# Pre-norm state-space layer and top-1 expert layer on one core: one of four tiles of each block turned by DMA, three steps placed elsewhere

## The reference

```python
x = L0_attn_x                                    # (2, 4096, 512)
n = layernorm(x)
s = sigmoid(silu(n @ s_w1.T + s_b1) @ s_w2.T + s_b2)
u = (n @ B_w.T + B_b) * s                        # (2, 4096, 128)
h_t = h_{t-1} @ A.T + u_t                        # scan over 4096 steps
y = h @ C_w.T + C_b + n @ D_w.T + D_b
x1 = x + y * sigmoid(n @ g_w.T + g_b)
m = layernorm(x1)
e = argmax(m @ gate_w.T)                         # one of 8 experts per row
out = x1 + m + m @ expert_w[e].T
```

## Time and profile before

| what | value |
|---|---|
| median of 3 timed runs | 926.9 us (925.25 to 929.12) |
| profiled execution: its own time | 928.0 us |
| its span, mean granted TensorE clock | 926.3 us, 0.996 |
| TensorE busy | 904.1 us (98%) |
| VectorE busy | 704.2 us (76%) |
| ScalarE busy | 597.2 us (64%) |
| GpSimd busy | 389.8 us (42%) |
| chain that ended last | 88% TensorE, 3% VectorE, 1% ScalarE |

### The profile page before, as it was taken

How to read it: one execution, slowest core, us unless ns; L and a number is a source line. 1 busy time by engine, 2 the same in 40 slices (tenths; PEclk the granted TensorE clock), 3 DMA queues, 4 the chain that set the end, 5 groups by cost and what they waited for, 6 DMA issues and landing times.

```text
span 926.3 us, 15829 instructions
## 1 busy us (share of the span) xinstructions
PE 904.1 (98%) x4565; PEld 739.5 (80%) x4566; DVE 704.2 (76%) x1725; ACT 597.2 (64%) x826; POOL 389.8 (42%) x492
## 2 busy tenths in 40 slices
PE   8999999999999999999999999999999999999995
PEld 7777888888888888888888888888868887888884
DVE  6778979788888979788888979788787465555552
ACT  5568676857767675867767685857534345666661
POOL 1032536181634536181634527181623453333432
PEclk9999999999999999999999999999999999999998
DMA  8435384746657474748557485846789868999881
GB/s 311 131 91 140 89 206 114 205 108 171 151 140 187 89 198 120 204 111 171 153 137 186 90 199 118 206 113 178 254 275 413 336 234 243 224 218 219 192 187 39
DMA packets 203593, 165.55 MB, mean 179 GB/s; under 512 B 128245, under 2 KB 161781, under 8 KB 202496
## 3 DMA queue, kind: packets, MB, share of 16 engines
q1 hardware_dynamic: 192576, 130.89, 55.6%
q0 software_dynamic: 10800, 33.70, 10.7%
q10 hardware_dynamic: 144, 0.07, 0.0%
HBM read 81.63 MB, written 54.68 MB: 147 GB/s over the span
## 4 chain that ended last, share of the span: by engine, by line
PE 88%; DVE 3%; issue 2%; SPq 1%; ACT 1%; DMA 1%; POOL 0%; ACTq 0%; DVEq 0%; POOLq 0%
PE y L1662 19%; PE y L1382 7%; PE y L1383 7%; PE y L1384 7%; PE gates L1382 7%; PE gates L1384 6%; PE gates L1383 6%; PE scan L1527 3%; PE turned L1568 3%; PE gates L1568 3%; PE scan L1382 2%; PE scan L1383 2%; PE scan L1384 2%; PE turned L1650 2%; PE scores L1484 2%
## 5 line engine op out<-in xcount | busy, mean ns | idle before, releaser
L1662 PE MATMUL y<-experts,x1T_hi 128*128 x568 | 180.7, 399 | 2.6 <-issue 2.5
L578 POOL TENSOR_SCALAR ln_var_eps<-ln_mean_var 128x4 f32<-128x4 f32 x16 | 3.6, 224 | 302.3 <-DVE ln_mean_var L1017 302.2
L1662 PEld LDWEIGHTS y<-experts,x1T_hi 128*128 128x128 f32 x568 | 103.4, 188 | 24.1 <-issue 4.2
L623 POOL DMA_INDIRECT out<-gate,ids x71 | 72.0, 1015 | 111.1 <-DVE gate L1347 68.2
L1662 PE MATMUL y<-experts,x1T_lo 128*128 x284 | 111.4, 392 | 0.0
L1347 DVE TENSOR_TENSOR gate<-y,raw_weights 128x512 f32<-128x512 f32 x71 | 49.1, 691 | 75.6 <-PE y L1662 50.4
L1382 PE MATMUL gates<-GwT_hi,xT_hi 128*128 128x512 f32 x256 | 104.6, 409 | 0.0
L1382 PE MATMUL y<-DwT_hi,xT_hi 128*128 128x512 f32 x256 | 101.8, 398 | 0.5 <-DVE gateT L939 0.5
L731 ACT ACTIVATE joined<-flipped 128x1024 uint16<-128x1024 uint16 x60 | 82.3, 1371 | 29.7 <-DVE xT_lo L1167 21.1
L1383 PE MATMUL y<-DwT_lo,xT_hi 128*128 128x512 f32 x256 | 100.3, 392 | 0.0
L1384 PE MATMUL y<-DwT_hi,xT_lo 128*128 128x512 f32 x256 | 100.3, 392 | 0.0
(11 more groups left out here) (276 smaller groups left out, 2340.9 us busy)
## 6 DMA issues: line engine op xcount, KB each, us to landing
raw_weights<-routed_rows SPq DMA_DIRECT2D x71, 258.0 KB
x_in<-L_attn_x SPq DMA_DIRECT2D x32, 512.0 KB, 5.0
x_rows<-L_attn_x SPq DMA_DIRECT2D x32, 512.0 KB, 4.9
turned_experts<-raw_weights SPq DMA_DIRECT2D x32, 512.0 KB, 5.3
experts<-turned_experts SPq DMA_DIRECT2D x8, 2048.0 KB
raw_weights<-L_ffn_expert_w SPq DMA_DIRECT2D x32, 256.0 KB, 3.1
routed_rows<-padrow SPq DMA_DIRECT2D x9, 258.0 KB
out<-gate,ids POOLq DMA_INDIRECT x71
```

What stands on the lines that cost most here:

```text
L623: nc.gpsimd.indirect_dma_start(out=out_rows, out_offset=bass.IndirectOffsetOnAxis(ap=ids[r][:, 0:1], axis=0), in_=res[r], in_offset=None, ...
L1662: ins = nc.tensor.matmul(Y[m % 2][:], x2T[a][:, k, m % 2 * P:(m % 2 + 1) * P], flat[:, bass.ds(first + (w * KD + k) * D, D)], start=(k == ...
```

## The change

In the bodies of blocks 2 to 14 (the tails of blocks 1 to 13):

- Tile 3 of x1 is no longer turned by TensorE. ScalarE splits it in planes (`halve_x1`), SyncE issues one more DMA transpose ahead of the next block's flips, ScalarE joins it (`join_x1`), and `tail_hi` and `tail_lo` read the joined tile in SBUF instead of a PSUM bank.
- On TensorE the first pair's last four score products stand alone; the second pair's products and `tail_back` move behind `to_middles` and behind the last `y_dense`; `over(b, 3)` to `over(b, 5)` and the products around them change places.
- `gates(b-1, 3)` of ScalarE moves behind the first sigmoid of the silu; `join(b+1, 2)` moves behind the copies of h.
- `ln2_stats` of tile 3 moves up to stand ahead of `over(b, 0)`; `gate_sum(b, 1)`, `tail_lo(b-1, 3)`, `low(b+1, 0)` and `low_piece(b, 0)` move down.
- `add_identity` moves from VectorE to GpSimd, behind `scatter` (from block 1's body on).

```diff
+        def by_dma(b, i):
+
+            return 0 < b < LASTB - 1 and i == NT - 1
+        x1_halves = yb[:, 0, :].bitcast(u16)
+        x1_flipped = yb[:, 2, :].bitcast(u16).rearrange("p (c t) -> p c t", t=P)
+        x1_joined = yb[:, 0, :]
...
+                if by_dma(b - 1, NT - 1):
+                    sp.wait_ge(S_["x1_halves"], b - 1)
+                    sp.dma_start_transpose(x1_flipped, x1_halves).then_inc(x1_turned, 16)
...
+            def add_identity(b, j):
+
+                f = expert_piece(b, j)[1]
+                pool.wait_ge(w_loaded[j], 16 * (b + 1))
+                part = w_raw[j][:, f * P:(f + 1) * P]
+                nc.gpsimd.tensor_tensor(part, part, ident[:], ALU.add).then_inc(w_ident[j], 1)
...
+                if 0 < b < LASTB:
+                    for j in range(2):
+                        add_identity(b + 1, j)
...
+            def halve_x1(b, i):
+
+                act.wait_ge(S_["x1_ready"], NT * b + i + 1)
+                nc.scalar.activation(x1_halves.rearrange("p (h d) -> p h d", h=2), planes(xrow[b % 2][:, i, 0:D]), ACT.Copy
+                                     ).then_inc(S_["x1_halves"], 1)
+
+            def join_x1(b, i):
+
+                act.wait_ge(x1_turned, 16 * b)
+                nc.scalar.activation(planes(x1_joined), x1_flipped.rearrange("p (h k) t -> p h (k t)", h=2), ACT.Copy
+                                     ).then_inc(S_["x1_joined"], 1)
...
-                    gates(b - 1, NT - 1)
...
+                    if tail and m == 0:
+                        gates(b - 1, NT - 1)
...
+                if dma:
+                    halve_x1(b - 1, 3)
...
+                if dma:
+                    join_x1(b - 1, 3)
+                    tail_hi(b - 1, 3)
...
+                if dma:
+                    gates(b, 1)
                 if tail:
                     scoresT(b - 1, 1)
-                gates(b, 1)
...
-                    join(b + 1, 2)
+                    if not dma:
+                        join(b + 1, 2)
...
+                if dma:
+                    ln2_stats(old, oldq, 3)
                 over(b, 0)
...
-                if tail and ahead:
-                    for j in range(2):
-                        add_identity(b + 1, j)
                 over(b, 3)
-                gate_sum(b, 1)
+                if not dma:
+                    gate_sum(b, 1)
                 over(b, 4)
+                if dma:
+                    gate_sum(b, 1)
...
+                if dma:
+                    tail_lo(old, 3)
...
+                elif tail:
+                    for n in range(KD, 2 * KD):
+                        score_product(b - 1, 0, n)
...
+                else:
+                    over(b, 3)
+                    gates(b, 1, 2, 3)
+                    over(b, 4)
+                    y_dense(b, 3, 0, 1)
+                    over(b, 5)
+                    y_dense(b, 3, 2)
+                    gates(b, 2, 0)
+                    to_middles(b)
+                    gates(b, 2, 1)
+                    tail_scores(b - 1, 1)
+                    gates(b, 2, 2, 3)
+                    down(b)
+                    y_dense(b, 3, 3)
+                    tail_back(b - 1, 1)
```

More of the change, by code:

```diff
@@ L789, in body @@
                     tail_hi(b - 1, 2)
+                if tail and not dma:
                     tail_hi(b - 1, 3)
+                if tail:
                     scoresT(b - 1, 0)
-                    if ahead:
-                        join_piece(b, 0)
+                if dma:
+                    join_x1(b - 1, 3)
+                    tail_hi(b - 1, 3)
+                if tail and ahead:
+                    join_piece(b, 0)
                 if ahead:
@@ L1172, in body @@
                 tail, ahead = b > 0, b < LASTB
+                dma = by_dma(b - 1, NT - 1)
                 old, oldq, oldturn = b - 1, 1 - q, turn - (1 - q)
@@ L1231, in body @@
                 over(b, 2)
-                if tail:
+                if tail and not dma:
                     tail_lo(old, 3)
-                if tail and ahead:
-                    for j in range(2):
-                        add_identity(b + 1, j)
                 over(b, 3)
-                gate_sum(b, 1)
+                if not dma:
+                    gate_sum(b, 1)
                 over(b, 4)
-                if tail and ahead:
+                if dma:
+                    gate_sum(b, 1)
+                if tail and ahead and not dma:
                     low_piece(b, 0)
@@ L1245, in body @@
                 over(b, 5)
-                if ahead:
+                if dma:
+                    tail_lo(old, 3)
+                elif ahead:
                     low(b + 1, 0)
@@ L1250, in body @@
                 to_middles(b)
+                if dma:
+                    low(b + 1, 0)
                 gate_sum(b, 2)
@@ L1268, in body @@
                     place(old, oldq, oldturn)
-                    ln2_stats(old, oldq, 3)
+                    if dma:
+                        low_piece(b, 0)
+                    else:
+                        ln2_stats(old, oldq, 3)
                 if ahead:
@@ L1444, in y_dense @@
                     if i == NT - 1:
-                        wait(pe, S_["x2T_lo"], NT * b)
+                        wait(pe, S_["x2T_lo"], NT * (b - 1) + 2 if by_dma(b - 1, NT - 1) else NT * b)
                 dense(Y[i], i, DwT, ks, False)
@@ L1603, in body @@
                 to_chunks(b)
-                if tail:
+                if tail and not by_dma(b - 1, 2):
                     tail_turn(b - 1, 1 - q, 2, True)
+                elif tail:
+                    for n in range(KD):
+                        score_product(b - 1, 0, n)
                 gates(b, 0, 1, 2)
                 over(b, 0)
-                if tail:
+                if tail and not by_dma(b - 1, 3):
                     tail_turn(b - 1, 1 - q, 3, True)
+                elif tail:
+                    for n in range(KD, 2 * KD):
+                        score_product(b - 1, 0, n)
                 gates(b, 0, 3)
```

48 lines of the change are left out of this document (30 added, 18 removed).

## The result

The changed kernel takes 932.24 us (median of four runs, 930.57 to 932.55); the kernel before, run beside it, 927.02. The ratio is 1.0061 [1.0045, 1.0076]: slower by 5.2 us. The prediction, 924.0 with a range to 930.5, was wrong. Its profiled execution took 930.6 us with a span of 928.7; that of before 928.0 with 926.3.

The account below looks back on a forecast made before the run. TensorE, busy for all 41.70 us of a block, was taken to bound the kernel. The terms -5.8 + 1.6 + 0.6 + 0.7 = -2.9 us, from 926.9, gave 924.0 us, with a range from 920.3 to 930.5.

Parts of the forecast that it names:

- The part that gives: TensorE's four transposes of tile 3: taking them away gives 0.445 us a block, 5.8 us over thirteen blocks.
- What is added, and where it is covered: ScalarE's halving (1.06 us) and joining (1.38 to 1.41) fit into idle time, with 2.3 us of cover at second `scoresT`.
- What becomes tight: the scan: VectorE's chains for the steps after `over(b, 3)` and `over(b, 4)`: 0.12 us of stall a block, 1.6 us in all.
- The scattered stops: ScalarE stops for something outside the core's engines; one of two or three will show: 0.7 us, bounds 0 and 3.
- What becomes tight: the last `high`: Next block's `s1` waits for xT_hi from ScalarE: 0.05 us a block, 0.6 us in all, bounds 0 and 2.1.
- How little is enough?: At the first scan matmul, a result there 0.15 us ahead is enough; below that, a third to all missing is stall.
- The rule against the change: GpSimd's identity addition may hold VectorE's `over(b, 0)` chain through a shared SBUF port: 0.34 us a block, 4.4 us; chance 0.12.
- The whole gain: Rival: the three tight places hold and TensorE keeps all 5.8 us, 921.1 us; chance 0.28.
- the late flip: Rival: the input's last DMA flip lands late, delaying ScalarE's join and `s1`; up to 935.7 us; chance 0.15.

Follow-up runs that it names:

- e8: e6 with TensorE's four transposes of tile 3 done as well and not read; 930.2 us, blocks of 41.83 us.
- e6: e2 with GpSimd's `add_identity` held back until the block's first gate sum; 923.64 us, ratio 0.9973 to before.
- e5: e2 with `add_identity` back on VectorE, ahead of `over(b, 3)`; 923.14 us, ratio 0.9974 to before.
- e3: The changed kernel with `add_identity` back on VectorE, ahead of `over(b, 3)`; one run, 929.7 us.
- e9: The kernel before with three idle ScalarE copies (two 128x512, one 128x8) ahead of the last `high` of blocks 3 to 14; 931.88 us, ratio 1.0069.
- e2: The changed kernel with ScalarE's `high(b+1, 1)` and `halve(b+1, 3)` moved ahead of the second `scoresT`; ratio 1.0005 to before.
- e1: The changed kernel with GpSimd's residual multiplication and addition cut from 512 to 8 columns; one run, 923.3 us.
- e7: The kernel before with two idle 128x512 ScalarE copies ahead of the last `high` of blocks 3 to 14; 926.09 us, ratio 1.0002.
- e10: The changed kernel with one idle 128x4 GpSimd instruction ahead of the residual of blocks 1 to 13; 927.95 us, ratio 1.0033 to before.

## Why the prediction was wrong

**The part that gives** was right: predicted 0.445 us a block, measured 0.46 (e8 less e6).

**What is added, and where it is covered** was right where it was costed. `halve_x1` ran at 369.22, in the idle time of the earlier trace rows, the join found its data landed, and ScalarE stood 2.56 us ahead of the second `scoresT` where 2.3 was predicted.

**What becomes tight: the scan** was right. The rows of after at `over(b, 4)`:

```profile
383.14 0.28 DVE L1021 TENSOR_TENSOR chunk_ends<-z,chunk_ends 128x112 fp32r<-128x112 f32 x1
...
383.47 0.36 PE L1595 MATMUL scan<-chunk_ends,A_powers_hi 128*128 128x192 f32 x1
...
383.66 0.27 PE L1595 MATMUL scan<-chunk_ends,A_powers_lo 128*128 128x192 f32 x1
```

The chain ends at 383.42. The first matmul comes 0.05 us behind it, and 0.28 behind the matmul before it where 0.23 is usual; the second comes 0.19 behind the first, where before had 0.09. That is about 0.14 us (0.13 in e6), the sum had 0.12; at `over(b, 5)` nothing clear is lost.

**The scattered stops** did not show: of blocks 3 to 14 none of after is over 42.12 us and none of e6 over 41.46. Of the 0.19 us (e8 less before) that leaves about 0.05 for which no place was found. So the two terms, (1.6 + 0.7) / 13 = 0.18 us a block, were right in sum, the second by luck. The forecast of 924.0 us comes near to what e6 measures, 923.64 beside a before of 926.05, but e6 is not the changed kernel: it has the early `high` and the late identity.

**What becomes tight: the last `high`** is the step that failed. It asked when TensorE's `s1` needs xT_hi, found about nothing to spare and took 0.05 us, 0.6 in all. Measured, the last `high` ended at 396.92, 0.43 ahead of `s1`, and TensorE did not wait. But VectorE's last `low` waits for the same `high`, and behind it in VectorE's queue stands the whole start of the block; the prediction named only one of the two that wait. The 0.38 us by which `low` slid gave the loss of 0.62 us a block (e5 against e3, e9 for its mechanism).

**How little is enough?** read the distance of 0.15 us between z's low piece and the first scan matmul, and used it as a yardstick for the other steps. It was itself the tightest of the block's scan steps (the next in the trace of before, `over(b, 4)`, has 0.25), in rows that were there, and was never put on the list. VectorE's three stops ahead of it, 0.80 us, would have looked like cover; the meeting took 1.29 + 0.14. What less than 0.15 does, the rows of after show: with 0.10 to 0.11 us the first matmul is still on time (`over(b, 1)` and `over(b, 5)`, 0.23 behind the one before), though at `over(b, 1)` the second comes 0.06 late; with 0.05 both are late (`over(b, 4)`).

**The rule against the change** was weighed for one place, the added identity beside `over(b, 0)`. That meeting is real (e2: 0.59 instead of 0.30, 0.31 us a block), but in after the scan is late already and it costs 0.07. The same meeting at the start of the block was already in the trace of before, in subtractions of one shape that lasted 0.68 (`low` at 353.06), 1.05 and 1.29; the question that these durations put was not asked. The Trainium skill ("SBUF — State Buffer", Who interferes with whom) says that a VectorE instruction with two SBUF inputs contends with a GpSimd instruction that reads SBUF, and that the order of issue decides who stands back. The traces here agree: 0.01 us ahead, 0.69 for VectorE and 1.84 for GpSimd; 0.05 behind, 1.80 and 1.29. GpSimd's power does not fit: it started 0.02 us ahead of `low` and was still the one that lasted longer (1.61 instead of 1.05).

**The rivals.** The whole gain didn't come; the late flip didn't either: ScalarE waited for a flip twice in the whole of after, 1.4 us at the longest, and in the block read not at all. The loss was on none of the lists.

## What to carry to other kernels

When an instruction of one engine becomes later, list all that wait for it, not only the engine that bounds the kernel, and follow what stands behind each in its queue. If one shape has several durations in the trace of before, find what decides between them before you move anything: a shift of 0.05 us in the order of two engines can be worth more than the instructions that a change removes. An idle time that a change opens ahead of a wait (here 2.56 us on ScalarE) is the place for the work that the change made late.

## What the runs showed of the hardware

- A VectorE subtraction of 128x512 from SBUF, 0.69 us alone (e1), lasts 0.69, 0.82, 1.05 or 1.80 us, by where it starts against GpSimd's 128x512 instructions. Started 0.05 us behind a GpSimd addition it lasts 1.11 us longer; started 0.01 us ahead, the addition lasts 0.55 longer instead.
- Worked out from the rows shown: the one that starts second lasts longer by what the first still has to run, less 0.13 to 0.14 us. VectorE second: 1.24 to run and 1.11 lost (after), 1.14 and 1.00 (e7's odd block), 0.50 and 0.36 (before). GpSimd second: 0.68 and 0.55 (e7), 0.54 and 0.40 (e10).
- The lengthening keeps itself going: with the first low piece late, the second (1.72) and GpSimd's next products (1.74 and 1.76 at 361.72 and 364.79 of after, 1.30 without) meet in the same way.
- A power of only 128x4 on GpSimd took 1.61 us when VectorE's 128x512 subtraction started 0.02 us behind it, and 1.05 when that started 0.23 us or more behind it (e7, after). Here the one that started first lasted longer; why was not tested.
- Added work made the kernel faster: one GpSimd instruction of 0.23 us in after, 0.3 us a block (e10).
